# A four-layer hybrid block on one core: a new order of work in the beginning, first maxima from tiles filled on chip, weights converted in pieces

## The chip, the cores and the metric

The kernel runs on one NeuronCore of one Trainium2 chip. The core has TensorE (matrix products into PSUM, eight banks of 128 x 512 fp32), VectorE, ScalarE and GpSimd, a sync engine (SP) that issues most transfers, and 16 DMA engines that the queues of SP and ScalarE share. The metric is device time in microseconds for one launch. In the rows, PE is TensorE's matmuls, PEld its weight loads, DVE VectorE, ACT ScalarE, POOL GpSimd, SPq and ACTq the issuing of transfers on SP and ScalarE.

## What is computed

`x` is 2 x 1024 tokens of 128 channels. Four layers, each added to x after a layer norm:

```python
x = x + attn_a(layernorm(x))    # 16 heads, each two softmax maps over 1024 keys (4 channels a map), a1 - lam * a2,
                                # RMS norm of the head's 8 outputs, projection
x = x + ffn(layernorm(x))       # shared expert + top 8 of 64 experts, silu(x @ W_up[e]) @ W_down[e], gated
x = x + attn_b(layernorm(x))    # softmax over 16 heads from one 128 x 128 energy per batch
x = x + ffn(layernorm(x))
```

In `attn_a`, `s = q k^T * scale`, `p = softmax(s)`, `out = p v` for 2 batches x 32 maps of 1024 x 1024 scores. This part lasts until about 655 us and holds all that the change touches.

## The kernel before

**Groups and steps.** Four maps (R = 4) are worked on together, each in a strip of 32 partitions, so there are 16 groups (NG), 8 for each batch. A group has 16 steps (QPG): two halves of the queries, eight key tiles each; NQ = 256 steps in all. The softmax is done with keys on partitions, so the row maximum must be known beforehand: a first pass of matmuls with queries on partitions (`m_items`, L1296) writes 128 x 1024 scores into two PSUM banks, and VectorE reduces them to the negated maximum (`max_quad`, L1067). A group has 32 such maxima, 512 in all, two a step. They run LEAD = 12 steps ahead of the scores of the same number (`quad_items`), so there are twelve steps of maxima alone, 244 of both, and twelve of scores alone.

**A strip's rows.** Queries and keys are split into three bf16 parts (high, middle, low). A strip stacks six slots of 4 rows, which pair parts of q with parts of k (Q_SLOTS, K_SLOTS), and behind them rows for the shift: keys there are one, and queries get the three parts of the negated maximum, so the score comes out with the maximum subtracted. The stacks are laid out in DRAM (`q_stack`, `k_stack`; `write_parts`, L479, one transfer of 256 KB a slot, twelve a batch), and read back into QB and KB for the scores (`load_strips`, L499) and into QA and KA for the maxima (`load_max`, L506 and L510). The transfers ScalarE issues for KA of group 0 are at L837.

**The shift.** When 16 maxima of a half are done, GpSimd splits them (`shift_parts`, L641 to L647), TensorE transposes them (`shift_tile`, L1305) at the end of step 8h - 3 (`shift_at`), VectorE copies them to SHT behind its first max of that step (L1080), and SP moves them to DRAM (`shift_d`, L530), waits for that, and reads them into the four strips of QB (L535, four transfers). The first scores of half h (step 8h, L1333) wait for these.

**A step** on TensorE (`quad`): scores 0, max, scores 1, now and then a transposed output tile, half of the weighted values of the step before (L1360), scores 2, max, scores 3, the shift's transpose if it is due, the other half of the weighted values. ScalarE takes the exponential of each 128 x 512 score tile into PR (L860); the tiles use four PSUM banks. At two steps in each half ScalarE also copies out the output sums (OTS, OSB).

**The beginning.** x is loaded in four chunks of 512 tokens. For each chunk VectorE takes statistics and, one chunk later, normalises (L1014); GpSimd computes the inverse roots. TensorE transposes the chunk (L1239), ScalarE copies it to XT (L796), TensorE projects queries and keys of the chunk before (L1249), ScalarE makes the high part (L814), VectorE the rest R1 (L1024), ScalarE the middle part (L818), VectorE the low part (L1029). Values (L1255) for all four chunks follow, then centroids. SP writes the stacks of batch 0 as each part of its two chunks is there, loads QA, fills and writes batch 1, and loads group 1; QB, KB of group 0 come last. ScalarE converts the experts' down weights (WDH), loads 2 MB of up weights in four transfers (RAWU), converts them at once (WUH, L847), and then starts the exponentials. PR lies over PARTS, so it also waits for both batches' stack writes (st_w).

**The end.** From step NQ - 12 on, SIDE lists the work on the first chunk of the expert layer beside the last scores: heads_T, proj, norm, x_T, affinity, top, sum and at NQ - 3 gate_T, whose result goes to DRAM (`gate_d`) and comes back as GATE (L573). The experts start behind the last step; `gated` (HF, L1108) needs GATE.

## Time and profile before

| | |
|---|---|
| three runs: median (lowest to highest) | 1083.62 us (1078.84 to 1085.8) |
| the profiled execution | 1082.55 us |
| its span | 1080.8 us |
| busy: TensorE, VectorE, ScalarE, GpSimd | 1001.8, 958.7, 890.6, 482.7 us |
| shares of the chain that ended last | VectorE 51%, TensorE 33%, ScalarE 5%, DMA 4%, issue 4% |

The span is what the profile covers of one execution. A busy time is the sum over the span, which has stages with different limits; the chain of waits is followed back from the last instruction, at each step to what released it. Where a row has brackets, they hold the idle time of the engine just before it and what ended it. A median time to landing counts from a transfer's issue to its completion.

### The profile page before, as it was taken

The page shows a single profiled execution, that of the slowest core. Times are in us where ns is not written, and L with a number is a line of the kernel's source. Part 1 is how long each engine was busy: PE and PEld are TensorE (multiplying, and loading weights), DVE is VectorE, ACT ScalarE, POOL GpSimd, SP SyncE. Part 2 cuts the span into 40 slices and gives each one's busy share as a digit, 9 for nine tenths or more (in the row PEclk, how much of TensorE's full clock was granted, in tenths as well). Part 3 has the DMA queues.
Part 4 walks back from the last instruction along what each step waited for, and adds up shares of the span by engine and source line. Part 5 has one row for each costly group of instructions (what it writes and reads, how often), then busy time and mean ns, then how long its engine had stood idle before and what let it go on. Part 6 is the DMA issues. An engine that isn't in the chain of part 4 may idle for free.

```text
span 1080.8 us, 21671 instructions
## 1 busy us (share of the span) xinstructions
PE 1001.8 (93%) x8016; PEld 517.0 (48%) x8016; DVE 958.7 (89%) x1187; ACT 890.6 (82%) x1466; POOL 482.7 (45%) x892
## 2 busy tenths in 40 slices
PE   6389999999999999999999999999999999999998
PEld 3012222232222222222222236888777778787876
DVE  7799999999999999999999956989876978797665
ACT  4279999999999999999999987878865787688765
POOL 3363555455445645564555657443412331333331
PEclk9569999999999999999999999999999999999999
DMA  8911110111011011101110007585766566757773
GB/s 276 306 34 51 52 51 4 51 51 32 23 52 51 17 37 52 51 3 51 52 52 3 22 3 171 151 195 146 173 179 156 137 161 174 194 153 188 197 187 91
DMA packets 80474, 108.91 MB, mean 101 GB/s; under 512 B 23537, under 2 KB 33521, under 8 KB 80369
## 3 DMA queue, kind: packets, MB, share of 16 engines
q1 hardware_dynamic: 66336, 100.98, 35.0%
q10 hardware_dynamic: 14032, 6.55, 2.4%
q8 instruction: 64, 1.05, 0.4%
q14 instruction: 42, 0.34, 0.1%
HBM read 95.57 MB, written 11.93 MB: 99 GB/s over the span
## 4 chain that ended last, share of the span: by engine, by line
DVE 51%; PE 33%; ACT 5%; DMA 4%; issue 4%; SPq 1%; POOL 0%; ACTq 0%; DVEq 0%; POOLq 0%
DVE NEGMAX L1067 46%; PE PS L1458 9%; PE PS L1460 8%; PE PS L1459 8%; PE PS L1360 3%; ACT PR L860 2%; PE PS L1333 1%; DVE HF L1108 1%; DVE HL L1116 1%; DMA shift_d<-SHT 1%; DMA GATE<-gate_d 1%; ACT PS L957 1%; ACT HH L950 1%; PE PS L1239 1%; DVE XC L1014 1%
## 5 line engine op out<-in xcount | busy, mean ns | idle before, releaser
L1067 DVE TENSOR_REDUCE NEGMAX<-PS 128x1 f32<-128x1024 f32 x512 | 584.9, 1211 | 10.2 <-PE PS L1296 9.9
L860 ACT ACTIVATE PR<-PS 128x512 f32<-128x512 f32 x1024 | 539.0, 600 | 36.7 <-PE PS L1333 24.7
L1360 PE MATMUL PS<-PR,VG 128*32 128x256 f32 (+1 forms) x3840 | 321.9, 407 | 17.3 <-ACT PR L860 2.0
L1333 PE MATMUL PS<-QB,KB 32*128 32x512 bf16 x1024 | 260.1, 387 | 3.6 <-DMA QB<-shift_d 2.1
L1296 PE MATMUL PS<-KA,QA 32*128 32x512 bf16 x1024 | 204.6, 397 | 30.7 <-DVE NEGMAX L1067 22.5
L1108 DVE TENSOR_TENSOR HF<-PS,GATE 128x1024 f32<-128x1024 f32 x128 | 156.3, 1222 | 65.0 <-ACT PS L957 55.2
L957 ACT ACTIVATE PS<-PS 128x1024 f32<-128x1024 f32 x128 | 129.2, 1009 | 75.5 <-PE PS L1460 74.4
L1333 PEld LDWEIGHTS PS<-QB,KB 32*128 32x128 bf16 x1024 | 75.2, 91 | 240.5 <-ACT PR L860 138.7
L950 ACT ACTIVATE HH<-HF 128x1024 fp32r<-128x1024 f32 (+1 forms) x136 | 139.8, 1029 | 24.2 <-DVE HF L1108 23.1
L769 POOL TENSOR_TENSOR HL<-HF,HH 128x1024 fp32r<-128x1024 f32 (+1 forms) x31 | 66.8, 2154 | 165.5 <-ACT HH L950 165.5
L1360 PEld LDWEIGHTS PS<-PR,VG 128*32 128x32 f32 x3840 | 76.4, 108 | 130.7 <-issue 65.0
L1116 DVE TENSOR_TENSOR HL<-HF,HH 128x1024 fp32r<-128x1024 f32 (+1 forms) x105 | 131.9, 1257 | 7.6 <-ACT HH L950 7.5
L1458 PE MATMUL PS<-XH,WUH 128*128 128x512 f32 x256 | 107.8, 421 | 0.0
L1458 PE MATMUL PS<-HH,WDH 128*128 128x512 f32 x256 | 102.5, 400 | 2.5 <-ACT YS L967 2.5
L1460 PE MATMUL PS<-HH,WDL 128*128 128x512 f32 x256 | 101.5, 396 | 0.0
L1459 PE MATMUL PS<-XL,WUH 128*128 128x512 f32 x256 | 101.4, 396 | 0.0
L1460 PE MATMUL PS<-XH,WUL 128*128 128x512 f32 x256 | 101.1, 395 | 0.0
L1459 PE MATMUL PS<-HL,WDH 128*128 128x512 f32 x256 | 100.8, 394 | 0.0
L675 POOL TENSOR_TENSOR ORC<-OSB,MINUS 128x16 f32<-128x16 f32 x32 | 93.2, 2911 | 3.3 <-DVE OSB L1093 0.9
L641 POOL TENSOR_TENSOR SHP<-NEGMAX,ZERO 128x16 bf16<-128x16 f32 x32 | 7.0, 218 | 167.2 <-DVE NEGMAX L1067 167.1
L1296 PEld LDWEIGHTS PS<-KA,QA 32*128 32x128 bf16 x1024 | 48.3, 91 | 58.5 <-DVE NEGMAX L1067 45.1
L1458 PEld LDWEIGHTS PS<-HH,WDH 128*128 128x128 f32 x256 | 48.4, 189 | 15.4 <-ACT YS L967 4.6
(186 smaller groups left out, 971.6 us busy)
## 6 DMA issues: line engine op xcount, KB each, us to landing
GATE<-gate_d SPq DMA_DIRECT2D x256, 256.0 KB, 4.2
QA<-q_stack SPq DMA_DIRECT2D x64, 128.0 KB, 2.6
QB<-q_stack SPq DMA_DIRECT2D x16, 256.0 KB, 3.0
KB<-k_stack SPq DMA_DIRECT2D x16, 256.0 KB, 3.0
KA<-k_stack SPq DMA_DIRECT2D x60, 64.0 KB, 2.4
q_stack<-PARTS SPq DMA_DIRECT2D x12, 256.0 KB, 4.4
k_stack<-PARTS SPq DMA_DIRECT2D x12, 256.0 KB, 4.2
RAWU<-in_L_ffn_W_up_dram ACTq DMA_DIRECT2D x4, 512.0 KB, 11.6
```

The lines of the kernel that those rows point to most:

```text
L860: nc.scalar.activation(PR[:, s % PRING, r, :], PS[:, SCORE_BANK[n], :], ACT.Exp, scale=SCALE_A).then_inc(p_ready, 1)
L950: nc.scalar.activation(HH[:, k, 0:u, :], HF[:, f, 0:u, :], ACT.Copy).then_inc(hh_ok, 1)
L957: nc.scalar.activation(PS[:, z:z + 2, :], PS[:, z:z + 2, :], ACT.Silu).then_inc(silu_ok, 1)
L1067: nc.vector.tensor_reduce(NEGMAX[:, hs % 2, col:col + 1], PS[:, e:e + 2, :].rearrange("p b n -> p (b n)"), axis=AX_X, op=ALU.max, negate=T ...
L1108: nc.vector.tensor_tensor(HF[:, k, :, :], PS[:, z:z + 2, :], GATE[:, h % GSLOTS, :, :], op=ALU.mult).then_inc(hf_ok, 1)
L1116: nc.vector.tensor_tensor(HL[:, k, 0:u, :], HF[:, f, 0:u, :], HH[:, k, 0:u, :].bitcast(F32), op=ALU.subtract).then_inc(hl_ok, 1)
L1296: last = mm(PS[:, e + h, :], QA[lo:lo + STRIP, u, r // 2, nt * P:(nt + 1) * P], KA[lo:lo + STRIP, u, r // 2, :], start=True, stop=True)
L1333: mm(PS[:, SCORE_BANK[n], :], KB[strip, u, mt * P:(mt + 1) * P], QB[strip, u, half * BANK:(half + 1) * BANK], start=True, stop=True).then_ ...
L1360: last = mm(PS[STRIP * r:STRIP * (r + 1), 7, cols], VG[:, u, mt, r // 2, :], PR[:, s % PRING, r, cols], start=mt == 0, stop=mt == TB - 1 a ...
L1458: mm(dst, ah, bh, start=first, stop=False)
L1459: mm(dst, ah, bl, start=False, stop=False)
L1460: return mm(dst, al, bh, start=False, stop=last)
```

## The change

- **Order of the beginning.** X chunks 0 and 1 are loaded ahead of WQKV and WPRJ. Ten bf16 matmuls on constants are added on TensorE (`warm`), four as soon as the constants are there and six behind the weights' transposes. The first projection runs as soon as chunk 0 is transposed, and the projections, transposes and copies of all chunks are interleaved in a written-out order; values of chunks 0 and 1 stand between chunks 1 and 2, those of 2 and 3 at the end. The low parts of chunks 0, 2 and 3 move to GpSimd. R1 has four buffers instead of two.
- **First 16 maxima from QB and KB.** VectorE fills QB and KB of buffer 0 with zeros and ones; SP copies the rows of all four strips of group 0 from PARTS into them, twelve transfers of 16 rows, as each part is there. The first half's maxima use these; from the second half on, QA and KA. Both of a max's matmuls then run on the same strip (before on two different ones).
- **Stacks.** The layout becomes channel by slot, so one transfer writes all slots of one part: six a batch instead of twelve. They are issued behind the twelve row transfers; the small loads (LAM, BPROJ, ...) behind them. KA of group 0 is loaded by SP. QB and KB of group 0 aren't loaded from the stacks any more.
- **Direct shifts.** SHP and SHT hold the parts strip by strip, with a fourth, zero part, and one transfer moves SHT straight into slot 7 of QB, without `shift_d`. The transpose stands at step 8h - 2 in the middle of the step (before scores 2).
- **Up weights in pieces.** RAWU is loaded in 16 transfers, one behind each of the first 16 shift transfers. ScalarE converts 512 columns at each of steps 28, 44, ... 140, GpSimd makes the low part of each piece. The bias is added to X by GpSimd in half 3 instead of ahead of the loop.
- **Eleven steps of lead** instead of twelve; the side work up to gate_T starts one step later (gate_T at NQ - 2).
- lambda's products move from VectorE to GpSimd; ScalarE converts the shared weights after it has waited for their loads (ld_exp), which SP issues behind group 1's loads.

```diff
-SHIFT_ROW = HD_A * len(Q_SLOTS)
 STRIP = 32
-STACK_WRITES = 16 * 2 * (len(Q_SLOTS) + 1)
+SLOTS = STRIP // HD_A
+SHIFT_SLOT = SLOTS - 1
+STACK_WRITES = 16 * 2 * 4
+FIRST_LOADS = 16 * 2 * len(Q_SLOTS)
...
-LEAD = 12
+LEAD = 11
...
-    return (g + 3) // TB if (g + 3) % TB == 0 and 0 <= (g + 3) // TB < 2 * NG else None
+    return (g + 2) // TB if (g + 2) % TB == 0 and 0 <= (g + 2) // TB < 2 * NG else None
...
-A_ITEM = ring_order(["wT"] + [("xT", c) for c in range(NCH)] + [("va", c) for c in range(NCH)] + ["centT"])
+A_ITEM = ring_order(["wT", ("xT", 0), ("xT", 1), ("xT", 2), ("va", 0), ("va", 1), "centT", ("xT", 3), ("va", 2), ("va", 3)])
+A_LATE = A_ITEM["va", 2]
...
+UP_PIECES = 8
+UP_PARTS = 2 * UP_PIECES
+
+
+def up_piece(s):
+
+    k = (s - 28) // QPG
+    return k if s >= 28 and (s - 28) % QPG == 0 and k < UP_PIECES else None
...
-    NQ - 12: [("heads_T", 0)], NQ - 11: [("proj", 0), ("stats", ("f", 0))], NQ - 10: [("norm", ("f", 0))],
-    NQ - 8: [("x_T", ("f", 0))], NQ - 7: [("affinity", 0)], NQ - 6: [("top", 0)], NQ - 5: [("sum", 0)], NQ - 3: [("gate_T", 0)],
+    NQ - 11: [("heads_T", 0)], NQ - 10: [("proj", 0), ("stats", ("f", 0))], NQ - 9: [("norm", ("f", 0))],
+    NQ - 7: [("x_T", ("f", 0))], NQ - 6: [("affinity", 0)], NQ - 5: [("top", 0)], NQ - 4: [("sum", 0)], NQ - 2: [("gate_T", 0)],
...
-        SHP = sb("SHP", [P, 2, 3 * SHIFTS], BF16, where=attn)
-        SHT = sb("SHT", [3 * SHIFTS, 2, P], BF16, where=attn)
+        SHP = sb("SHP", [P, 2, R, 4, SHIFTS // R], BF16, where=attn)
+        SHT = sb("SHT", [4 * SHIFTS, 2, P], BF16, where=attn)
...
+            load_x(0)
+            load_x(1)
+            sp.dma_start(WQKV[:], w_qkv.rearrange("(j p) c -> p j c", p=P)).then_inc(ld_w, 16)
+            sp.dma_start(WPRJ[:], w_proj).then_inc(ld_w, 16)
+            load_x(2)
+            load_x(3)
+            sp.wait_ge(const_ok, 2)
...
+                    step = places[1] - places[0] if len(places) > 1 else 1
+                    rows = stack[b * GPB:(b + 1) * GPB].rearrange("g r d c n -> (g r d) c n")[:, places[0]:places[-1] + 1:step, :]
+                    sp.dma_start(rows, src.unsqueeze(1).to_broadcast([P, len(places), SEQ])).then_inc(st_w[b], 16)
+
+            def first_rows(part, j):
+
+                tile, slots = ((QB, Q_SLOTS), (KB, K_SLOTS))[j]
+                for c in [c for c, a in enumerate(slots) if a == part]:
+                    sp.dma_start(tile[c:P:SLOTS, 0, :], PARTS[0:R * HD_A, part, j, 0:SEQ]).then_inc(first_ld, 16)
...
             fill_shift_rows(0)
+            sp.dma_start(CENT[:], cent).then_inc(ld_b, 16)
+            for j, w in enumerate((w_q, w_k, w_v, w_o)):
+                sp.dma_start(WB[:, j, :], w).then_inc(ld_b, 16)
+            sp.wait_ge(first_set, 2)
+            for part, made in enumerate((qk_hi, qk_mid)):
+                for j in range(2):
+                    sp.wait_ge(made, 2 * NCH // BATCH - 1 + j)
+                    first_rows(part, j)
+            for j in range(2):
+                sp.wait_ge(qk_lo_pool, j + 1)
+                sp.wait_ge(qk_lo, j + 1)
+                first_rows(2, j)
+            for part in range(3):
+                write_parts(0, part)
...
             sp.wait_ge(st_w[0], STACK_WRITES)
-            load_max(0, 0, False)
+            load_max(0, 0)
+            fill_shift_rows(1)
+            for part, (made, n) in enumerate(((qk_hi, 2 * NCH), (qk_mid, 2 * NCH), (qk_lo_pool, 6))):
+                sp.wait_ge(made, n)
+                write_parts(1, part)
+            load_max(1, 1)
+            sp.wait_ge(const_ok, 3)
             sp.dma_start(RAWSU[:, 0:F], ws_up).then_inc(ld_exp, 16)
             sp.dma_start(RAWSD[0:F, :], ws_down).then_inc(ld_exp, 16)
-            fill_shift_rows(1)
-            write_stacks(1)
-            load_max(1, 1)
-
             sp.wait_ge(st_w[1], STACK_WRITES)
-            load_strips(q_stack, QB, 0, 0, sh_w)
-            load_strips(k_stack, KB, 0, 0, kb_ld[0])
+
+            def load_up(part):
+
+                es = slice(part * E // UP_PARTS, (part + 1) * E // UP_PARTS)
+                sp.dma_start(RAWU[:].rearrange("d (e f) -> d e f", f=F)[:, es, :],
+                             w_up[es, :, :].rearrange("e d f -> d e f")).then_inc(ld_up, 16)
 
             def shift_rows(s, half):
 
                 u, hs = s % 2, 2 * s + half
+                if half == 0 and s:
+                    sp.wait_ge(sh_w, 16 * s)
                 sp.wait_ge(sht_ok, hs + 1)
-                sp.dma_start(shift_d[half].rearrange("a r (t n) -> (a r t) n", n=P), SHT[:, half, :]).then_inc(sh_w, 16)
-
-                sp.wait_ge(sh_w, 48 * s + 16 * (half + 2))
-                for r in range(R):
-                    lo = STRIP * r + SHIFT_ROW
-                    sp.dma_start(QB[lo:lo + 3, u, half * BANK:(half + 1) * BANK], shift_d[half, :, r, :]).then_inc(sh_r, 16)
+                sp.dma_start(QB[SHIFT_SLOT:P:SLOTS, u, half * BANK:(half + 1) * BANK], SHT[:, half, :]).then_inc(sh_r, 16)
...
+                    if s < UP_PIECES:
+                        load_up(2 * s + half)
...
+            def low_part(c):
+
+                cols = slice(c * BANK, (c + 1) * BANK)
+                for j in range(2):
+                    n = D_ITEM["qk", j, c]
+                    pool.wait_ge(qk_mid, n + 1)
+                    nc.gpsimd.tensor_tensor(PARTS[:, 2, j, cols], R1[:, n % 4, :], PARTS[:, 1, j, cols], op=ALU.subtract).then_inc(qk_lo_pool, 1)
+
             for c in range(NCH):
                 root_of(("a", c))
+            for c in (0, 2, 3):
+                low_part(c)
...
+            transposed(0)
+            high_part(0, 0)
+            transposed(1)
+            high_part(1, 0)
+            middle_part(0, 0)
+            high_part(0, 1)
+            high_part(1, 1)
+            middle_part(1, 0)
+            middle_part(0, 1)
+            middle_part(1, 1)
+            transposed(2)
+            values(0)
+            values(1)
+            centroids()
+            high_part(0, 2)
+            transposed(3)
+            high_part(1, 2)
+            middle_part(0, 2)
+            middle_part(1, 2)
+            high_part(0, 3)
+            high_part(1, 3)
+            middle_part(0, 3)
+            middle_part(1, 3)
+            values(2)
+            values(3)
             act.wait_ge(ld_down, 16)
             nc.scalar.activation(WDH[:], RAWD[:], ACT.Copy).then_inc(w_hi, 1)
-            for part in range(4):
-                load_up(part)
-            act.wait_ge(ld_exp, 32)
-            act.wait_ge(ld_up, 16 * 4)
-            for dst, src in ((WUH, RAWU), (WSUH, RAWSU), (WSDH, RAWSD)):
-                nc.scalar.activation(dst[:], src[:], ACT.Copy).then_inc(w_hi, 1)
             act.wait_ge(lam_in, 1)
             nc.scalar.activation(lam_e[:], lam_s[:], ACT.Exp).then_inc(lam_exp, 1)
+            act.wait_ge(ld_exp, 32)
+            for dst, src in ((WSUH, RAWSU), (WSDH, RAWSD)):
+                nc.scalar.activation(dst[:], src[:], ACT.Copy).then_inc(w_hi, 1)
+            act.wait_ge(first_ld, FIRST_LOADS)
...
+                act.wait_ge(ld_up, 16 * UP_PARTS // UP_PIECES * (k + 1))
+                nc.scalar.activation(WUH[:, cols], RAWU[:, cols], ACT.Copy).then_inc(w_hi, 1)
...
+            nc.vector.memset(QB[:, 0, :], 0.0).then_inc(first_set, 1)
+            nc.vector.memset(KB[:, 0, :], 1.0).then_inc(first_set, 1)
             for c in range(NCH):
                 dve.wait_ge(ld_x[c], 16)
                 stats(("a", c))
-                if c:
+                if 1 <= c <= 2:
                     norm(("a", c - 1))
-            norm(("a", NCH - 1))
-            for c in range(NCH):
-                rest_and_low(c)
-            dve.wait_ge(ld_mix, 16 * 9)
-            for j in range(2):
-                link(nc.vector.tensor_tensor(lam_p[:, j, :], LAM[:, 2 * j, :], LAM[:, 2 * j + 1, :], op=ALU.mult))
-            nc.vector.tensor_reduce(lam_s[:], lam_p[:], axis=AX_X, op=ALU.add).then_inc(lam_in, 1)
-            link(nc.vector.tensor_scalar(SUBW[:], SUBW[:], 1.0 - LAMBDA_INIT, None, ALU.mult))
-
+            rest(0, 0)
+            norm(("a", 2))
+            rest(1, 0)
+            rest(0, 1)
+            rest(1, 1)
+            low_part(0, 1)
+            low_part(1, 1)
+            norm(("a", 3))
...
+                for _ in range(times):
+                    mm(PS[:, 7, :], identb[:], ONES[:, 0:BANK], start=True, stop=True)
...
+            warm(4)
...
+            warm(6)
+            transposed(0)
+            copied(0)
+            query_or_key(0, 0)
+            transposed(1)
+            query_or_key(1, 0)
+            copied(1)
+            query_or_key(0, 1)
+            query_or_key(1, 1)
+            transposed(2)
+            values(0)
+            values(1)
+            centroids()
+            copied(2)
+            query_or_key(0, 2)
+            query_or_key(1, 2)
+            transposed(3)
+            copied(3)
+            query_or_key(0, 3)
+            query_or_key(1, 3)
+            values(2)
+            pe.wait_ge(first_ld, FIRST_LOADS)
...
+                    if hs == 0:
+                        strip = slice(STRIP * r, STRIP * (r + 1))
+                        for h in range(2):
+                            last = mm(PS[:, e + h, :], QB[strip, 0, nt * P:(nt + 1) * P],
+                                      KB[strip, 0, h * BANK:(h + 1) * BANK], start=True, stop=True)
+                        last.then_inc(m_full, 1)
+                        if it == 1:
+                            values(3)
+                        continue
+                    if a == 0 or hs == 1:
```

## Rows read from the trace of the kernel before

**Rows 1.** The page: lines of the chain that ended last, and a group of instructions.

```profile
DVE NEGMAX L1067 46%; PE PS L1458 9%; PE PS L1460 8%; PE PS L1459 8%; PE PS L1360 3%; ACT PR L860 2%; PE PS L1333 1%; DVE HF L1108 1%; DVE HL L1116 1%; DMA shift_d<-SHT 1%; DMA GATE<-gate_d 1%; ACT PS L957 1%; ACT HH L950 1%; PE PS L1239 1%; DVE XC L1014 1%
...
L1067 DVE TENSOR_REDUCE NEGMAX<-PS 128x1 f32<-128x1024 f32 x512 | 584.9, 1211 | 10.2 <-PE PS L1296 9.9
```

**Rows 2.** Stretches: length, busy us per engine, TensorE's granted clock, DMA share, GB/s.

```profile
36.00:50.00 14.00, 6.92 (x26) 1.13 (x23) 13.72 (x13) 0.00 (x0) 8.49 (x1) 0.50 1.13 359
...
150.00:250.00 100.00, 95.14 (x1038) 29.49 (x1034) 99.85 (x94) 94.77 (x186) 51.59 (x121) 1.00 0.15 42
```

**Rows 3.** Timelines (start, us, instruction, releaser) around two shifts; last row: transfers of SHT.

```profile
261.02 0.20 DVE L1080 COPY SHT<-PS 48x128 bf16<-48x128 bf16 x1
...
261.15 16.01 DVE L1067 TENSOR_REDUCE NEGMAX<-PS 128x1 f32<-128x1024 f32 x14
...
261.25 0.31 SPq L530 DMA_DIRECT2D shift_d<-SHT  x1
...
265.62 0.38 PE L1333 MATMUL PS<-QB,KB 32*128 32x512 bf16 x1
...
279.57 0.32 SPq L530 DMA_DIRECT2D shift_d<-SHT  x1
...
297.89 0.31 SPq L530 DMA_DIRECT2D shift_d<-SHT  x1
...
300.31 1.18 SPq L535 DMA_DIRECT2D QB<-shift_d  x4
...
DMA to landing us min/median/max: 1.3/1.4/2.9
```

**Rows 4.** Timelines of the first maxima and the first scores.

```profile
35.63 0.61 PE L1296 MATMUL PS<-KA,QA 32*128 32x512 bf16 x4 [7.89 <-DMA KA<-k_stack]
...
36.28 4.62 DVE L1067 TENSOR_REDUCE NEGMAX<-PS 128x1 f32<-128x1024 f32 x4 [7.21 <-PE PS L1296]
...
62.16 0.58 PE L1333 MATMUL PS<-QB,KB 32*128 32x512 bf16 x1
...
69.05 1.22 DVE L1067 TENSOR_REDUCE NEGMAX<-PS 128x1 f32<-128x1024 f32 x1 [0.89 <-PE PS L1296]
```

**Rows 5.** Timelines of the projections, 0 to 40 us.

```profile
10.00 1.11 DVE L1014 TENSOR_SCALAR XC<-X,ln_mv,ln_inv 128x128 f32<-128x128 f32 x4
...
24.65 1.29 DVE L1024 TENSOR_TENSOR SQ<-PS,PARTS 128x512 f32<-128x512 f32 x2
...
21.17 1.08 ACT L814 ACTIVATE PARTS<-PS 128x512 bf16<-128x512 f32 x2
...
25.38 1.23 ACT L818 ACTIVATE PARTS<-SQ 128x512 bf16<-128x512 f32 x2 [0.58 <-DVE SQ L1024]
...
12.07 3.62 PE L1249 MATMUL PS<-XT,WT 128*128 128x512 f32 x4
...
21.33 1.99 PE L1249 MATMUL PS<-XT,WT 128*128 128x512 f32 x4 [0.60 <-ACT XT L796]
```

**Rows 6.** An issue on SP, DMA issues (last number: us to landing), a conversion on ScalarE.

```profile
51.91 0.60 SPq L506 DMA_DIRECT2D QA<-q_stack  x1
...
RAWSD<-in_L_ffn_Ws_down_dram SPq DMA_DIRECT2D x1, 32.0 KB, 4.4
...
57.30 3.62 ACT L847 ACTIVATE WUH<-RAWU 128x4096 fp32r<-128x4096 f32 x1 [21.70 <-DMA RAWU<-in_L_ffn_W_up_dram]
```

**Rows 7.** Waits, 80 to 620 us: total us, times, longest us.

```profile
DVE NEGMAX L1067 <- PE PS L1296: 1.3, 5, 0.3
```

**Rows 8.** Timelines from the last maxima into the experts.

```profile
624.72 0.56 PE L1333 MATMUL PS<-QB,KB 32*128 32x512 bf16 x2
...
653.65 0.50 PE L1458 MATMUL PS<-XH,WUH 128*128 128x512 f32 x1
...
652.09 21.97 SPq L573 DMA_DIRECT2D GATE<-gate_d  x18
...
658.60 2.35 DVE L1108 TENSOR_TENSOR HF<-PS,GATE 128x1024 f32<-128x1024 f32 x2
```

More of the change, by code:

```diff
@@ L116, in score_tiles @@
                 tiles["out", output_at(g)] = len(tiles)
-        if shift_at(g) is not None:
-            tiles["shift", shift_at(g)] = len(tiles)
+            if p == 1 and shift_at(g) is not None:
+                tiles["shift", shift_at(g)] = len(tiles)
     return tiles
@@ L864, in exp_quad @@
                         copy_out(output_at(s))
+                if up_piece(s) is not None:
+                    high_up(up_piece(s))
             def evac_out(k):
@@ L1281, in _, with copied, values, centroids @@
-            pe.wait_ge(identb_ok, 1)
+            def copied(c):
+                pe.wait_ge(a_free, A_ITEM["xT", c] + 1)
+            def values(c):
+                n = A_ITEM["va", c]
+                if n >= A_LATE:
+                    pe.wait_ge(qk_r1, D_ITEM["qk", n - A_LATE, 2] + 1)
+                else:
+                    pe.wait_ge(a_free, n - 3)
+                tokens(XT, WT[:, 2, :], c)(a_bank(n)).then_inc(a_full, 1)
+            def centroids():
+                n = A_ITEM["centT"]
+                pe.wait_ge(ld_b, 16 * 5)
+                pe.wait_ge(a_free, n - 3)
+                nc.tensor.transpose(PS[:, a_bank(n), 0:E], CENT[:], ident[0:E, 0:E])
+                nc.tensor.transpose(PS[:, a_bank(n), E:E + DIM], WB[:, 2, :], ident[:]).then_inc(a_full, 1)
@@ L1377, in quad @@
                     weighted_values(s - 1, 0)
+                if shift_at(s) is not None:
+                    shift_tile(shift_at(s))
                 if scored:
```

219 lines of the change are left out of this document (99 added, 120 removed).

## Prediction

> **What bounds the kernel now.** I read the page first: its chain of waits gives 46% of the span to the row maxima of L1067, the largest share of any line, and its groups say 512 maxima at 1211 ns, with only 10.2 us of idle VectorE before them [rows 1]. The stretches agree: from 150 to 250 us VectorE is busy 99.85 us, TensorE 95.14, ScalarE 94.77 [rows 2]. One half group (8 steps, 16 maxima) lasts 279.57 - 261.25 = 18.32 us. Fourteen maxima take 16.01, so one takes (16.01 - 1.21)/13 = 1.14 and sixteen 18.2; the SHT copy adds 0.13 [rows 3]. So up to the last max, time is "when the first max starts, plus 512 x 1.14, plus holes". The timelines give the two ends of that run. The first max starts at 36.28 [rows 4], although the last middle part of queries and keys is ready at 26.6 [rows 5]: ten us go into writing stacks to DRAM and reading them back, and TensorE waits 7.89 on KA [rows 4]. After the last max, twelve steps of scores alone run from 624.72 to 653.65 (28.9 us, 2.4 a step), then the experts [rows 8]. So three places can pay: the wait ahead of the first max, the number of steps without maxima, and holes.
>
> **The sum** is made against the profiled execution, 1082.55 us (span 1080.8). The median shown is 1083.62, 0.1% more, a difference I leave standing.
>
> **Start of the maxima.** Normalisation is bound as before by GpSimd's roots; chunk 1 is normalised at 11.1 [rows 5], chunk 0 one chunk (2.4) earlier, at 8.7. TensorE no longer holds the first projection back for the second transpose. Its first four projection records took 3.62 us, the last four 1.99 [rows 5]: 1.8 against 0.95 a projection. The ten added matmuls of warm() cover 4 to 9 us, and I take 0.95 from the first projection on (the other end: 4 x 0.85 = 3.4 us later, of which ScalarE's queue hides about half). The Trainium skill (TensorE: Matmul & The Clock Gate, Part 1: The HAM clock gate) has the engine throttled by default and released by activity; the drop from 3.62 to 1.99 agrees.
>
> ScalarE is then the long pole. Two PSUM copies take 1.08 with their overlap, so 0.5 each in a row; a middle part takes 0.61 [rows 5]. The first high part is done at 11.5, then by the new order T1 12.2, high 13.2, middle 13.8, two highs 15.0, three middles 16.8. T2, two values and the centroids end at 18.8; two highs, T3 and two middles at 22.0, because T3 waits until 19.6 for norm 3, now behind two low parts on VectorE. Two highs end at 23.0, VectorE's last two rests, 0.65 each [rows 5], at 23.8. TensorE is through with values(2) at 23.0.
>
> The strips must be there too. The twelve row transfers start behind the third high part, 14.3. One issue costs 0.30 (QB<-shift_d, few rows) [rows 3] to 0.60 (QA, 64 rows) [rows 6]; sixteen rows is nearer the first, so 0.39 with the gap. The last waits for low parts on VectorE (17.5) and GpSimd (17.2), is issued at 19 and lands 1.4 to 2.9 later [rows 3]: 21 (with 0.60 issues 22 + 2.9 = 25). So VectorE starts the first max at **24.1** (24 to 26.5) instead of 36.28: **-12.2 us**. The maxima from QB and KB run their two matmuls on one strip, one after the other: 0.61 + 0.4 at the low clock where the parallel ones took 0.61 [rows 4], still under 1.14: nothing, at most 0.05 each, 0.8.
>
> **Supply of the other maxima.** Max 16 needs QA and KA at 24.1 + 18.2 = 42.3. SP issues six stack writes (3 MB) from 19 to 23.5; at the 359 GB/s of 36 to 50 us [rows 2] they are down at 29. Nine small loads end at 28.7; eight QA and KA issues run 29 to 34 and land by 38: 4 us to spare, 1 to 2 at the slow ends. Then 1 MB of fill and 3 MB of stacks, down at 46.5. Group 1's eight loads, RAWSU and RAWSD are queued behind and issued by 48.3. RAWU's 2 MB, which shared that stretch before, have moved into the loop.
>
> **First scores.** SHT follows 19 maxima, 24.1 + 21.5 = 45.6, as before, but SP reaches its transfer only at 48.3, behind group 1's loads and the wait for the second batch's stacks: landed at 49.8. TensorE was at step 0 25.9 us after the first max (62.16 [rows 4]); with one step less that is 23.6: 47.7. It is held 2.1 and has run 1.4 ahead of VectorE, part of which covers: **+1.4**. ScalarE waits for RAWSD, issued at 48, landing 4.4 later [rows 6], so exps start at 52: **+0.8**. TensorE at half clock (0.50 from 36 to 50 [rows 2]) let VectorE idle 0.89 in the first steps [rows 4]. The new run has no 7.9 us gap; whether the clock stays up isn't shown, so about half: **-0.5** (0 to -0.9).
>
> **Eleven steps of lead.** One of twelve steps without maxima goes, -2.4; the side work stays the same, +0.2: **-2.2**. The gate write keeps its distance from the last max, but the experts start 2.4 earlier. GATE was issued at 652.09 [rows 8]; with RAWSD's 4.4 to land [rows 6] it was there at 656.5, and the first HF ran at 658.60 [rows 8]: 2.1 to spare against 2.4, **+0.5**.
>
> **Direct shifts.** Before: SHT copy until 261.22, two transfers one behind the other, first score of the next half at 265.62 [rows 3]. Now the copy is a step (2.28) later and ends at 263.5; one transfer has 2.1 us. The landing took 1.3 to 2.9, median 1.4, in an odd half 300.31 - 297.89 = 2.4 [rows 3]. Normal halves are on time, some 0.3 late and mostly absorbed: **+0.5** (0 to 3). The Trainium skill (DMA: Bandwidth & Descriptors, Anatomy of one DMA) puts some 2.0 us of fixed cost on a transfer, most of it the confirmed write, measured on GpSimd's path. By that, an estimate, every shift would land on the limit; the median of 1.4 differs, and it is what the sum uses.
>
> **Pieces and GpSimd.** WUH in one piece took 3.62 in ScalarE's idle time [rows 6]; eight pieces of 0.45 plus 0.1 now stand in the loop. ScalarE is idle 5.2% there [rows 2], 0.96 a half, 1.9 a group. It is spread over the steps, so I count on half, 0.96 a group against 0.55: **+1** (0 to 4.4). VectorE waited for TensorE's maxima only 1.3 us from 80 to 620 [rows 7] although OTS and OSB interrupt the exps in every half. GpSimd is busy 51.6 of 100 [rows 2]: 8.8 idle a half hold the bias add (4.5) and low pieces (1.1): nothing; uncovered, 8 x 1.1.
>
> **Sum:** -12.2 + 1.4 + 0.8 - 0.5 - 2.2 + 0.5 + 0.5 + 1 = -10.7, so 1082.55 - 10.7 = 1071.9, said as **1072**.
>
> **Rivals.**
> - *The wait moves to SP.* Both stacks, group 1's loads and RAWSD stand ahead of the first shift and exp. With 0.60 issues for the twelve rows and slower writes the shift leaves at 53 and exps start at 57: 5 us of the gain go, 1077. Against: RAWU is away, the writes are six, not twelve.
> - *ScalarE becomes the bound.* Pieces at full price 4.4, and 0.1 on each of 32 halves 3.2: 7.6 in place of my 1.5, 1078. Against: [rows 7].
> - *Slower: the direct shift is late in every half.* Room is 2.1, ScalarE wins back 0.5, so it costs from a landing of 2.6. At the slowest row's 2.9 each half loses 0.3, 9.6 in all: 1081. From 3.0 it eats the gain (0.4 x 32 = 12.8): 1084; at 3.3, 22 and 1094. For: nothing stands behind the copy any more, and odd halves' 2.4. Against: the median of 1.4, and one target in DRAM less.
> - *All ends good:* first scores not held, clock up, pieces free, shifts on time: 1071.9 - 2.2 - 0.4 - 1 - 0.5 = 1067.8.
>
> **How the numbers follow.** The forecast's own case (1069.5 to 1075) gets 0.44, all good 0.12, SP 0.17, ScalarE 0.13, late shifts 0.14. A measurement of this kernel tells about 1% from no change, here 1072.8. Faster by over 1%: all good and 0.37 of the forecast's, 0.49. Within 1%, to 1094.5: its other 0.07, SP, ScalarE, half of late shifts, 0.44. Slower by over 1% needs landings of 3.3 and more throughout: 0.07. Range 1066 to 1080: outside are the late shifts and 0.06 of ends.
>
> **What would show it.** First max at 24 to 26 and none waiting for KA: the start is right; after 28, or a wait for QA at max 16, and the largest term is wrong. SHT of half 0 at 45.6, its transfer near 48: SP's queue; exps at 52: RAWSD. A half of 18.3: pieces and shifts are covered; 18.6 or more with TensorE waiting for QB<-SHT is the third rival, with VectorE idle at the steps of pieces the second. TensorE's clock from 25 to 50 tells the transition's cost; HF waiting for GATE behind the last score, the gate term.

## The result and the profile after

The changed kernel takes 1085.82 us (median of 19 runs, 1080.93 to 1092.37) where the kernel before, on the same chip, takes 1081.13 (19 runs): a ratio of 1.0040, with a 95% interval of 1.0027 to 1.0053. It is 0.4% slower; the forecast was 1072, with a range of 1066 to 1080. The profiled execution took 1087.36, with a span of 1085.6 against 1080.8, so the two traces differ by as much as the medians.

First the page of the changed kernel: the chain that ended last by line (cut), then the groups that answer to [rows 1].

```profile
DVE NEGMAX L1148 32%; ACT PR L929 7%; PE PS L1583 7%; PE PS L1585 6%; PE PS L1584 6%; PE PS L1485 6%; DMA GATE<-gate_d 4%; PE PS L1458 3%; DVE HF L1189 2%; DVE HL L1197 1%; SPq L496 1%; PE PS L1467 1%; PE PS L1320 1%; ACT HH L1021 1%; ACT PS L1028 1%
...
L1148 DVE TENSOR_REDUCE NEGMAX<-PS 128x1 f32<-128x1024 f32 x512 | 585.5, 1211 | 13.6 <-PE PS L1419 13.1
...
L1458 PE MATMUL PS<-QB,KB 32*128 32x512 bf16 x1024 | 262.7, 387 | 13.4 <-DMA QB<-SHT 9.7
```

The maxima are L1148 now (L1067 before), at the same 1211 ns. Two things are new. The maxima's own line holds 32% of the chain, not 46%. And the scores, L1458, have 9.7 us of idle TensorE in front of them that ended with the transfer of shifts, QB<-SHT. Where that stands, the timelines of the head tell (start, us, instruction, idle before and its releaser; VectorE, TensorE and ScalarE first, then SP's queue):

```profile
25.42 22.10 DVE L1148 TENSOR_REDUCE NEGMAX<-PS 128x1 f32<-128x1024 f32 x19
47.43 0.21 DVE L1161 COPY SHT<-PS 64x128 bf16<-64x128 bf16 x1
59.92 4.62 DVE L1148 TENSOR_REDUCE NEGMAX<-PS 128x1 f32<-128x1024 f32 x4 [8.89 <-PE PS L1419]
65.59 10.38 DVE L1148 TENSOR_REDUCE NEGMAX<-PS 128x1 f32<-128x1024 f32 x9 [1.05 <-PE PS L1419]
75.89 0.21 DVE L1161 COPY SHT<-PS 64x128 bf16<-64x128 bf16 x1
...
59.18 0.60 PE L1458 MATMUL PS<-QB,KB 32*128 32x512 bf16 x1 [9.74 <-DMA QB<-SHT]
...
58.77 0.31 ACT L912 ACTIVATE WSUH<-RAWSU 128x128 fp32r<-128x128 f32 x1 [17.95 <-DMA RAWSD<-in_L_ffn_Ws_down_dram]
```

```profile
15.77 1.83 SPq L502 DMA_DIRECT2D QB<-PARTS  x3
...
28.38 1.24 SPq L496 DMA_DIRECT2D k_stack<-PARTS  x1
29.66 1.46 SPq L520 DMA_DIRECT2D LAM<-n_L_attn_a_lambda_q_dram  x1
...
35.74 0.49 SPq L536 DMA_DIRECT2D QA<-q_stack  x1
...
48.31 1.29 SPq L496 DMA_DIRECT2D k_stack<-PARTS  x1
49.65 1.33 SPq L536 DMA_DIRECT2D QA<-q_stack  x1
...
56.18 0.58 SPq L550 DMA_DIRECT2D RAWSU<-in_L_ffn_Ws_up_dram  x1
56.80 0.47 SPq L551 DMA_DIRECT2D RAWSD<-in_L_ffn_Ws_down_dram  x1
57.37 0.59 SPq L566 DMA_DIRECT2D QB<-SHT  x1
```

The first maximum starts at 25.42, 10.9 us earlier than in [rows 4], and none waits for KA. But SP's queue is never idle from 15.77 to 57.37: first rows, six writes, small loads, loads for maxima, fill and six writes more, the second group's loads, the shared weights. Only then does the transfer of shifts leave, ten us behind its copy at 47.43. TensorE's program can't pass its first scores, so the maxima behind them stop: VectorE stands still for 8.89 us, then 1.05.

The lead of the changed kernel at five landmarks shows where the time went. The columns are: landmark, before, after, after minus before (us of the two traces).

```
first maximum starts                 36.28    25.42   -10.86
SHT copy of half 0                   57.78    47.43   -10.35
SHT copy of half 1                   77.68    75.89    -1.79
SHT copy of half 31                 628.92   628.93    +0.01
gates of the first chunk (CWT)      649.13   651.17    +2.04
third HF of the experts             662.34   664.77    +2.43
end of the span                    1080.8   1085.6     +4.8
```

So 8.6 us are lost between halves 0 and 1, 1.8 in the loop, 2.4 from there into the experts and 2.4 in the experts.

### The profile page after: what moved, and what is told of

Same layout as the page of the kernel before. It is cut to its first block, busy times and chain, and to the rows that moved or that the text cites. A ratio compares the mean times of both kernels' runs of the same rounds, so it can differ in the third digit from the quotient of the medians.

```text
span 1085.6 us, 21613 instructions
## 1 busy us (share of the span) xinstructions
PE 1010.4 (93%) x8026; PEld 520.7 (48%) x8026; DVE 957.2 (88%) x1179; ACT 888.6 (82%) x1473; POOL 492.1 (45%) x911
## 3 DMA queue, kind: packets, MB, share of 16 engines
q8 instruction: 64, 1.05, 0.4%
## 4 chain that ended last, share of the span: by engine, by line
DVE 38%; PE 34%; ACT 11%; issue 5%; DMA 5%; SPq 5%; POOL 0%; DVEq 0%; ACTq 0%; POOLq 0%
DVE NEGMAX L1148 32%; ACT PR L929 7%; PE PS L1583 7%; PE PS L1585 6%; PE PS L1584 6%; PE PS L1485 6%; DMA GATE<-gate_d 4%; PE PS L1458 3%; DVE HF L1189 2%; DVE HL L1197 1%; SPq L496 1%; PE PS L1467 1%; PE PS L1320 1%; ACT HH L1021 1%; ACT PS L1028 1%
## 5 line engine op out<-in xcount | busy, mean ns | idle before, releaser
L1148 DVE TENSOR_REDUCE NEGMAX<-PS 128x1 f32<-128x1024 f32 x512 | 585.5, 1211 | 13.6 <-PE PS L1419 13.1
L1458 PE MATMUL PS<-QB,KB 32*128 32x512 bf16 x1024 | 262.7, 387 | 13.4 <-DMA QB<-SHT 9.7
L1419 PE MATMUL PS<-KA,QA 32*128 32x512 bf16 x992 | 194.6, 389 | 14.0 <-DVE NEGMAX L1148 12.8
L1458 PEld LDWEIGHTS PS<-QB,KB 32*128 32x128 bf16 x1024 | 78.4, 91 | 237.7 <-ACT PR L929 115.6
```

Of the source, the lines that this page charges most:

```text
L1148: nc.vector.tensor_reduce(NEGMAX[:, hs % 2, col:col + 1], PS[:, e:e + 2, :].rearrange("p b n -> p (b n)"), axis=AX_X, op=ALU.max, negate=T ...
L1419: last = mm(PS[:, e + h, :], QA[lo:lo + STRIP, u, r // 2, nt * P:(nt + 1) * P], KA[lo:lo + STRIP, u, r // 2, :], start=True, stop=True)
L1458: mm(PS[:, SCORE_BANK[n], :], KB[strip, u, mt * P:(mt + 1) * P], QB[strip, u, half * BANK:(half + 1) * BANK], start=True, stop=True).then_ ...
```

## Experiments

Each ratio below is to the kernel before, run on the same chip as the version (medians 1079.96 to 1081.09); the changed kernel's own is 1.0040. Where a version is set against the changed kernel, the difference by the ratios is the better one, since the chips are not the same.

The queue of SP first (e1). The first transfer of shifts goes ahead of the second group's loads, and the two shared weights leave with the small loads:

```diff
             sp.dma_start(EBIAS[:], e_bias.partition_broadcast(P)).then_inc(ld_mix, 16)
+            sp.wait_ge(const_ok, 3)
+            sp.dma_start(RAWSU[:, 0:F], ws_up).then_inc(ld_exp, 16)
+            sp.dma_start(RAWSD[0:F, :], ws_down).then_inc(ld_exp, 16)
...
+            shift_rows(0, 0)
             load_max(1, 1)
-            sp.wait_ge(const_ok, 3)
-            sp.dma_start(RAWSU[:, 0:F], ws_up).then_inc(ld_exp, 16)
-            sp.dma_start(RAWSD[0:F, :], ws_down).then_inc(ld_exp, 16)
             sp.wait_ge(st_w[1], STACK_WRITES)
```

> The changed kernel with another order on SP only: RAWSU and RAWSD are loaded with the small loads, the first shift's transfer stands right behind the second batch's stack writes, ahead of group 1's QA and KA. In the changed kernel the SHT copy ended at 47.6 us, its transfer was issued at 57.37 and VectorE idled 8.9. Theory A (SP's queue holds the first scores): transfer issued near 50, landed by 53 to 54 behind the stack writes, first exps at about 54 instead of 59.9, VectorE's hole 4 us or less; 5 us faster than the changed kernel, about 1080.5, level with the kernel before. Theory B (the hole is only paid elsewhere: the loop or the end wait anyway): first scores earlier, the end within 1 us of the changed kernel's 1085.8.

It took 1079.94 us, a ratio to before of 0.9984 (0.9968 to 1.0001), 5.9 us under the changed kernel (6.0 by the ratios). Its timelines of SP, TensorE and VectorE:

```profile
50.16 1.24 SPq L564 DMA_DIRECT2D QB<-SHT  x1
...
54.48 0.60 PE L1461 MATMUL PS<-QB,KB 32*128 32x512 bf16 x1 [5.30 <-DMA QB<-SHT]
...
55.22 4.61 DVE L1151 TENSOR_REDUCE NEGMAX<-PS 128x1 f32<-128x1024 f32 x4 [4.45 <-PE PS L1422]
...
71.87 0.21 DVE L1164 COPY SHT<-PS 64x128 bf16<-64x128 bf16 x1
```

The transfer leaves 7.2 us earlier and lands 4.3 us after its issue (the last stack write lands at 54.25, the transfer at 54.43), the hole halves, and the copy of half 1 comes at 71.87 instead of 75.89. Four us of the gain are seen here. The two traces differ by 3.3 us more, 1.7 between the last copy and the third HF and 1.6 in the experts; the first is a fall of TensorE's clock that e1's trace does not have (below), and neither is shown to come from the order of SP.

The counterpart (e9) delays the first maximum and leaves the queue as it is:

```diff
             pe.wait_ge(first_ld, FIRST_LOADS)
+            pe.wait_ge(st_w[0], STACK_WRITES)
```

> The changed kernel with one wait more: the first maximum's products also wait until the first batch's stack writes have landed (about 34 to 35 us), so that the first maximum ends at about 35 to 36 and not 25.4; nothing else is moved. Theory (the first scores and exponentials, at 59.2 and 59.9, wait for SP's queue and not for the maxima, and the maxima then lose 9 to 10 us of their lead by waiting for the scores): the 9.5 us of delay fit into the hole of 8.9 us in front of the thirteenth product pair and the second of about 1; time 0 to 2 us over the changed kernel, 1085.8 to 1088, the hole gone. Rival (the early start is worth what the sum gave it): 9 us and more over it, 1095.

Measured: 1086.99 us, ratio 1.0061 (1.0044 to 1.0079), 0.2% over the changed kernel by the ratios (2.3 us; 1.2 by the medians; six executions). VectorE's timeline:

```profile
34.30 2.36 DVE L1148 TENSOR_REDUCE NEGMAX<-PS 128x1 f32<-128x1024 f32 x2 [9.25 <-PE PS L1410]
...
57.20 7.99 DVE L1148 TENSOR_REDUCE NEGMAX<-PS 128x1 f32<-128x1024 f32 x7
...
76.69 0.21 DVE L1161 COPY SHT<-PS 64x128 bf16<-64x128 bf16 x1
```

The first maximum is 8.88 us later than in the changed kernel, the copy of half 1 only 0.80, and the hole of 8.89 is gone. So of the early start some 8 us are worth nothing at the copy of half 1 as long as the first scores wait: this is shown from both sides.

The lead (e2): twelve steps again, all side work one step back, the transpose of shifts at 8h - 2 as in the changed kernel.

```diff
-LEAD = 11
+LEAD = 12
```

> The changed kernel with twelve steps of lead and the side work up to gate_T back at its old steps; the shift's transpose stays at step 8h - 2. Theory A (the end is set by the chain heads_T to gate_T to GATE and by ScalarE, so a step less between the last max and the experts brings nothing): 0 to 3 us faster than the changed kernel, with HF no longer waiting for GATE (2.7 us in the first three). Theory B (my prediction's term: eleven steps save 2.2 us): 2 us slower than the changed kernel, about 1088.

1084.86 us, ratio 1.0029 (1.0010 to 1.0047): 1 us under the changed kernel, not told apart from it. Its first maximum started at 27.77 in the trace; its first HFs do not wait for GATE. Going from twelve steps to eleven bought nothing in all.

Then the transpose of shifts one step earlier beside it (e3):

```diff
-    return (g + 2) // TB if (g + 2) % TB == 0 and 0 <= (g + 2) // TB < 2 * NG else None
+    return (g + 3) // TB if (g + 3) % TB == 0 and 0 <= (g + 3) // TB < 2 * NG else None
```

> As the run before, and the shift's transpose at step 8h - 3, so the direct transfer has 4.4 us instead of 2.1 before the half's first scores. In the changed kernel's trace three transfers took 2.3, 2.9 and 3.6 us to land, and two halves lasted 19.06 and 19.76 us instead of 18.32. Theory A (late landings hold TensorE): no half over 18.6, 2 to 4 us faster than with the transpose at 8h - 2, and a smaller spread of the runs. Theory B (the holes are ScalarE's pieces): the same two halves stay long, no difference.

1082.58 us, ratio 1.0015 (0.9996 to 1.0033). Behind the first one (28.46, with the hole), half periods (SHT copy to SHT copy) of the changed kernel begin 18.32, 18.48, 18.32, 19.06, 18.33, 19.76, 18.32, 18.56; here, behind the first, no one is over 18.68. Two things changed at once, though. Only one of this trace's 32 transfers of shifts landed late at all (2.85 us, issued at 629.2), where e2's trace has six of 2.6 to 3.4, so most of the gain is that late landings are gone, not that they are absorbed. That a step more of time does absorb one is seen in four transfers, this one and one each in e5, e6 and e11 (2.2, 3.3 and 3.2 us): no score waited for them.

The pieces (e4): the eight conversions in the loop shrink to one column each; WUH is filled from other weights in ScalarE's idle time, so the up weights are not the right ones.

```diff
+            nc.scalar.activation(WUH[:], RAWD[:], ACT.Copy)
...
-                nc.scalar.activation(WUH[:, cols], RAWU[:, cols], ACT.Copy).then_inc(w_hi, 1)
+                nc.scalar.activation(WUH[:, k * BANK:k * BANK + 1], RAWU[:, k * BANK:k * BANK + 1], ACT.Copy).then_inc(w_hi, 1)
```

> The changed kernel, but ScalarE's eight conversions in the loop copy one column each instead of 512; WUH is filled from RAWD in ScalarE's idle time, so the experts' up weights are wrong numbers. The rest stays. Theory A (pieces cost what the trace shows, halves of 18.56 in place of 18.32 eight times): 2 us faster than the changed kernel. Theory B (ScalarE's idle time covers them, the long halves are from the transfers): no difference. Full price, 0.5 each: 4 us.

1083.61 us, ratio 1.0029 (1.0013 to 1.0046). By the ratios this is 1.2 us under the changed kernel, and the intervals overlap, so the price of the pieces is read from the trace: the later halves are 18.32 (one is 18.44) instead of 18.56 in every second one, so a piece costs 0.24 us and eight 1.9. Halves of 19.03, 19.41 and 19.64 remain: the late transfers are another cause.

For these I had two suspects: the load of up weights issued right behind the transfer, and instruction fetches. One edit (e8) moves the loads half a group away.

```diff
                 for half in range(2):
                     shift_rows(s, half)
-                    if s < UP_PIECES:
-                        load_up(2 * s + half)
                 if more:
                     sp.wait_ge(m_full, ITEM["max", QPG * s + QPG - 1, 1] + 1)
                     load_max(u, s + 2)
+                if s < UP_PIECES:
+                    load_up(2 * s)
+                    load_up(2 * s + 1)
```

> The changed kernel with one edit: the two loads of up weights (one piece of 16) of a group are issued behind the load of queries and keys for maxima, half a group away from both transfers of shifts. Theory U (the up weights' many small packets right behind the transfer of shifts make it land late): landings of the transfer of shifts at most 2.0, no half period above 18.6 after the first, time 2 to 2.5 us under the changed kernel: about 1083.5. Theory I (instruction fetch, seen as 0.02 MB on a queue of its own just before the late ones, delays the transfer): landings of 2.3 to 3.6 and half periods of 19.0 to 19.8 remain as they are, time same within 0.5 us: 1085.5 to 1086.

1083.69 us, ratio 1.0035 (1.0016 to 1.0053), not told apart from the changed kernel. Landings of 2.5, 2.9, 3.6 and 3.6 us remain, halves of 19.02, 19.71 and 19.79 too. The up loads are not the cause. The view of DMA traffic shows the other suspect at work. Two stretches of 5 us of the changed kernel, in 40 slices of 0.125 us, each from 1 us before an issue of QB<-SHT: first that of 168.68, then that of 206.76.

```profile
GB/s 0 0 0 0 0 0 0 0 0 0 0 0 0 0 0 0 0 14 95 14 131 0 6 111 203 199 232 137 70 37 12 8 10 10 16 6 0 0 66 0
...
q8 instruction: 1, 0.02, 1.2%
...
QB<-SHT SPq DMA_DIRECT2D x1, 16.0 KB, 3.6
...
GB/s 0 0 0 0 0 0 0 0 0 0 0 0 0 0 0 0 0 12 105 14 0 0 4 76 160 313 244 172 107 39 0 0 8 8 10 8 10 10 10 0
...
QB<-SHT SPq DMA_DIRECT2D x1, 16.0 KB, 1.7
```

The shifts' own bytes are the 14 95 14 and 12 105 14, 1.1 to 1.5 us behind the issue in both. In the first stretch one slice of 131 stands right behind them, an instruction fetch of 16 KB; the transfer lands after 3.6 us. In the second the fetch comes at +2.1, within the up weights' bytes, and it lands after 1.7. Over the traces of before and of twelve changed versions there are 416 transfers out of SHT:

```
instruction fetch starts, from issue    transfers    landing of 2.0 us or more
-0.3 to +1.5 us                             41           41 (2.0 to 3.6)
later, or none within 4 us                 375            5 (one with a fetch at +1.6; four behind stack writes)
```

The edge is sharp: 47 transfers had a fetch at +1.6 to +2.0, and only the one above was late. This is a coincidence found without exception in 41 cases, not an experiment that moved the fetch on purpose; the next one moved it by accident.

> The changed kernel without the ten products at the start (four and six) that only keep TensorE busy. Theory: without them the granted clock of TensorE is 0.5 for longer in the first 12 us, the first projection's and transposes' products take twice as long (1.06 instead of 0.60 for four transposes, 2.07 instead of 1.12 for a projection), the first maximum comes 2 to 3 us later (27.5 to 28.5), and since the first scores wait for SP's queue behind the same parts of queries and keys, half of it or all is passed on: 1085.8 to 1088.5. Rival (the head's clock rises by itself, as the spread of the first maximum from 25.1 to 27.8 between traces with these products suggests): first maximum 25 to 28 as before, the same time within 1 us.

In e10 the ten products are gone (`warm(4)` and `warm(6)`). It took 1085.17 us (ratio 1.0056, 1.0041 to 1.0071, five executions; 1.7 us over the changed kernel by the ratios). The first maximum is 0.7 us later, 26.13, not 2 to 3: the first projection does run at the lower clock (2.07 us for two records against 1.12), but little of that reaches the first maximum. What the ten products are worth stays open: e2 and e3 have them, and their traces too have the first projection at the lower clock, a granted clock that rises at 16 us (14.3 here) and a first maximum at 27.8. And with ten TensorE instructions less, the fetches near even transfers came at +1.7 us and later, no transfer landed in over 1.8, and behind the first (29.40) no half was over 18.57. The trace is of the fastest of the five executions (1080.41; the others 1084.4 to 1086.5), so whether the others had late transfers isn't known. That points to fetches of TensorE's own program, whose place against the transfer depends on how many instructions lie ahead.

The remaining versions look for a better order. The first, e5, has the edits of e1, e2 and e3 together.

> The three edits of the first experiments together: queue order of SP (first transfer of shifts before the second group's loads, shared weights with the small loads), twelve steps of lead, transpose of shifts one step earlier in the middle of its step. Theory (the loss is the first scores' wait, eleven steps pay nothing, and late transfers of shifts cost about 0.5 each only where the transpose is late): the parts add, 1085.8 - 5.9 (queue order) - 1.5 to -3 (late transfers absorbed) = 1077 to 1078.5, DVE's hole before the thirteenth maximum about 4.5 us, even half periods at most 18.7, HF without a wait for GATE. Rival (eleven steps do save their 2.2 us, and the queue order alone carried the gain): 1080 or more.

1077.08 us, ratio 0.9973 (0.9952 to 0.9994): as forecast by the sum of its parts, 8.7 us under the changed kernel (7.2 by the ratios) and 4.0 under the one before.

In e6 the small loads and shared weights go ahead of `sp.wait_ge(first_set, 2)`, into SP's idle time:

> e5 and one edit more: the nine small loads and the two shared weights are issued before the first rows, in the time in which SP's queue waits for the first parts of queries and keys (9.3 to 15.8 us in the changed kernel), and no longer between the stack writes of the two batches. Theory (SP's queue is what the first scores wait for, and what it issues before them counts one for one): 11 issues of about 0.6 leave the way, second batch's writes end 5 to 6 us earlier, first exponential at about 50 instead of 55, DVE's hole before its twelfth or thirteenth maximum at most 1 us, total about 4 us under e5: 1073 to 1075. Rival (the exponentials wait for something else by then, such as the writes' own bandwidth of 256 to 768 KB each, or for the transfer of shifts behind these writes): at most 1.5 us under e5.

1077.65 us, ratio 0.9978 (0.9956 to 0.9999): no gain. SP's queue of this version tells why:

```profile
29.14 1.26 SPq L496 DMA_DIRECT2D k_stack<-PARTS  x1
35.59 0.50 SPq L539 DMA_DIRECT2D QA<-q_stack  x1
```

Where the small loads had been, SP now waits 5.2 us for the first batch's writes to land. They had cost nothing there. In their new place they hold back the first rows, and the first maximum starts at 26.1 instead of 24.7. My expectation had taken SP's issues for the bound; at this place it is the landing of the first batch's writes: the DMA engines move 371 to 389 GB/s until 33 us, and the last write lands at 35.58.

Its counterpart e7 has e6's order and the changed kernel's eleven steps and transpose.

> The queue order of e1 and e6 with the changed kernel's own eleven steps of lead and its transpose of shifts at the end of the step. Theory (eleven steps bring nothing, and with no time left between transpose and scores the late transfers cost 0.5 to 1 each): 1 to 3 us slower than e6, even half periods of 19.0 to 19.8 two or three times, HF waits for GATE of about 1 us each. Rival (eleven steps save their step once the hole is gone): the same as e6 or up to 2.2 faster.

1079.31 us, ratio 0.9998 (0.9980 to 1.0017), 1.7 us over e6, with halves of 19.11, 19.06 and 19.63: twelve steps and the earlier transpose together are worth about that once the order is right, though the two intervals overlap.

The last one, e11, is e6 with 2.5 MB of the second batch's writes in that wait (the loop behind them loses its part 0):

```diff
+            fill_shift_rows(1)
+            sp.wait_ge(qk_hi, 2 * NCH)
+            write_parts(1, 0)
             sp.wait_ge(st_w[0], STACK_WRITES)
             load_max(0, 0)
-            fill_shift_rows(1)
```

> e6_loads_in_idle and one edit: the second batch's fill rows and first parts (2.5 of its 4 MB) are written before SP waits for the first batch's writes (30.4 to 35.5 us in e6, in which SP issued nothing and the DMA engines moved 2 to 27 GB/s for 3 us). Theory (in e6 the small loads only left a wait behind: the first scores wait for the bytes of both batches' stack writes, moved at 370 to 400 GB/s, and for SP's issues): transfer of shifts issued at about 48.7, right behind its copy, and landing in 2 us, not 4.5; exponentials at 51 to 52 instead of 54.6; the maxima's holes (0.15, 1.05 and three of about 0.35 in e6) gone: 1 to 2 us under e6's 1077.65, the maximum 17 perhaps late by up to 1.5 (queries and keys for maxima lie behind 2.5 MB). Rival (the maxima have been the bound in e6): the same within 1 us, though the exponentials start earlier.

1077.45 us, ratio 0.9968 (0.9951 to 0.9984), not told apart from e5 and e6. The transfer lands in 1.8 us, as expected, but exponentials start at 55.15, not at 51: its first maximum starts at 27.2 and its seventeenth waits 1.10, so that the copy of half 0 comes at 50.34. The time is the rival's, though the exponentials did not start earlier. No score waits for QB<-SHT in this trace, so the queue no longer holds the first scores. That the maxima themselves are the bound again fits this, but no run moved them alone behind this order.

## Why the prediction was wrong

**The start of the maxima** held: 25.42 for 24.1 (24 to 26.5). The step that was off is the price of one first-row issue: 0.39 by the nearer of two rows, 0.61 in the trace (1.83 for three), the upper end. From the first maximum to the SHT copy it is 22.01 us against 21.50 before, 0.5 more, inside the bound of 0.8 that the serial products had.

**First scores** is the step that failed. The sum put the first transfer's issue at 48.3 and the cost at 1.4 + 0.8 - 0.5 = 1.7; the issue came at 57.37, and 9.07 us were lost from the first maximum to the copy of half 1. The place and the mechanism were named (the first rival even had 53 and 57), the sizes were not. SP's queue up to the transfer, stretch by stretch (us):

```
                                             in the sum    in the trace
first row issue leaves at                       14.3          15.77
twelve row issues                                4.7           7.6
six writes of the first batch                    4.5           6.3
small loads, wait for the writes                 5.5           6.1
QA and KA of group 0                             5.0           5.0
fill and six writes of the second batch         12.5           8.9
group 1's loads, shared weights                  1.8           7.7
transfer of shifts leaves at                    48.3          57.37
```

Three terms were much too small, and one was 3.6 too large and hid part of that. The row issues took 0.61 each. The stack writes hold SP's queue for longer than the sum took, because only the first two take 0.58 and 0.48 and the next four, though smaller, 1.05 to 1.38. And the second group's loads, shared weights included, all stand between the last write and the transfer (49.65 to 57.37); I had read their place in the program but priced them as if they were issued while the writes were still moving. The order of SP is worth 4.0 us at the copy of half 1 (5.9 in the medians, e1), and without it 8.9 us of early start are worth 0.8 there (e9).

The two smaller terms beside it went as follows. RAWSD (+0.8) held nothing: it landed at 58.74, ahead of the first scores at 59.18. The half of the clock's loss that was to come back (-0.5) did not: the granted clock was 0.50 from 28.7 to 66.2 us, and VectorE waited 1.05 for products behind the first scores, where it was 0.89 before.

**Why the rest of the 1077 rival was off as well:** it gave up 5 of 12.2 us; the hole took 8.9, since every us by which the transfer is late beyond the run-ahead of the maxima counts in full.

**Eleven steps.** The step itself came off where forecast: from the last maximum's products to the first up product 29.8 us before (623.83 to 653.65), 29.25 after (624.16 to 653.41), and 1.5 of these belong to a fall of TensorE's granted clock:

```profile
620.00:636.00 16.00, 15.15 (x157) 1.00 0.01 3
636.00:640.00 4.00, 3.76 (x17) 0.57 0.00 0
640.00:656.00 16.00, 15.00 (x156) 1.00 0.06 16
```

(Stretch, length, TensorE's busy time, granted clock, DMA share, GB/s.) Over the other traces this comes out cleanly: with eleven steps and no such fall it is 27.7 us (e1, e4, e7, e10), with eleven and a fall at 636 to 641 it is 29.2 (this one, e8, e9), with twelve 29.7 to 29.9 (e2, e3, e5, e6, e11). So the step saved 2.1 us, -2.2 forecast, and in the profiled execution the fall took 1.5 of it back. Why the clock fell in three of seven stays open. But the **gate** term, +0.5, ate it all: the gates follow the last maximum, not the last score (CWT 20.2 us behind the last SHT copy before, 20.7 with eleven steps, 22.2 here with the fall), and HF, the first user, stands still. VectorE's timeline:

```profile
659.02 1.22 DVE L1189 TENSOR_TENSOR HF<-PS,GATE 128x1024 f32<-128x1024 f32 x1 [0.57 <-DMA GATE<-gate_d]
661.28 1.22 DVE L1189 TENSOR_TENSOR HF<-PS,GATE 128x1024 f32<-128x1024 f32 x1 [1.03 <-DMA GATE<-gate_d]
...
664.77 1.22 DVE L1189 TENSOR_TENSOR HF<-PS,GATE 128x1024 f32<-128x1024 f32 x1 [1.14 <-DMA GATE<-gate_d]
```

Three waits of 2.7 us, where the kernel before had none of them [rows 8]. The slack of 2.1 was counted for the first HF alone, and to the first of its two transfers. In the trace of before the second, fourth and sixth transfer land 1.9, 0.7 and 1.2 us ahead of the first three HFs; that is what there was to spare. From the last SHT copy to the third HF it is 33.4 us before, 33.4 to 34.3 with eleven steps and the clock up (e10, e7, e1, e4), 35.1 to 35.8 with the fall (e9, e8, this one): the net of both terms is nothing, not -1.7.

**Direct shifts:** +0.5 forecast, 1.9 measured (18.48 instead of 18.32, 19.06 and 19.76 instead of 18.56). The ordinary landing is 1.7 to 1.8 us, not the 1.4 that the DRAM path's first leg had, so a normal half is just on time and every one with a fetch is late. The spread of [rows 3] from 1.3 to 2.9 goes with the fetches too: in the trace of before all ten transfers of 2.0 us and more have a fetch at -0.3 to +0.9. The Trainium skill (DMA: Bandwidth & Descriptors, Anatomy of one DMA) puts about 2.0 us of fixed cost on a transfer that GpSimd issues; the 1.7 to 1.8 measured here on SP's queue is nearer to that than to my 1.4.

**Pieces:** +1 forecast, 1.9 measured. Half of ScalarE's idle time was to hide them; 0.24 us of each piece (0.55 by the sum) is not hidden. **Supply** held: no maximum waited for QA.

**The loop as a whole** came out near the forecast for a wrong reason. It is 1.8 us longer from the copy of half 1 to that of half 31, where the sum had 1.5. The two last terms cost 3.8; against that the kernel before lost 1.6 us over 18.32 a half, which the changed one does not, and the changed kernel's last half is 0.4 shorter. No term of the sum stood for either, so the agreement is luck.

**What stays open** is the last 2.4 us, in the experts. From the third HF to the end it is 418.5 us before and 420.8 after, but 416.6 to 424.4 in the other versions, whose experts are the same. Waits of HF for GATE sum to 9.0 us against 6.7, yet the version with 416.9 has 8.5. This stretch varies more from run to run than the difference, and no run here settles it.

## What to carry to other kernels

An earlier start is worth only what the next meeting of two streams lets through. Before pricing it, write out the whole issue queue that feeds that meeting, with the measured time of every issue, big writes above all, and see what stands ahead of the one transfer that decides. A transfer that must land within one step needs the slowest landing as its price; where it had one step more, four landings of 2.2 to 3.3 us held nothing. And shortening one tail helps only if what runs beside it (here the gates' transfers) is shortened too.

## What the runs showed of the hardware

- A DMA issue's time on SP's queue depends on what is already under way: the first stack writes of 768 KB take 0.58 and 0.48 us, the next ones of 512 and 256 KB 1.05 to 1.38, a load of a few KB behind them 1.46 (LAM) and a load for maxima 1.33, the same loads later 0.43 and 0.60. Without such a backlog three rows take 0.3, sixteen partitions of 2 KB 0.61.
- A transfer of 16 KB from SBUF to SBUF lands in 1.7 to 1.8 us. All 41 transfers of shifts with an instruction fetch of 16 KB that starts from 0.3 before to 1.5 us behind the issue took 2.0 to 3.6; of 47 with a fetch at +1.6 to +2.0, one did. In the two that were looked at closely the bytes moved at the same time. Where the fetches fall differed in the trace of a version with ten TensorE instructions less.
- TensorE's granted clock falls to half for 3.4 us at places that differ between traces of like code (at 636 to 638 us in three of seven versions with eleven steps, 1.5 us of time), and in the head rises at different times: at 9.0 to 11.6 us in four versions, whose first maximum started at 25.1 to 25.5, and at 16.0 and 16.2 in two with the same head, whose first maximum started at 27.8.
